# Queries from split half-precision operands, and normalised rows written by GpSimd, in layer 0 of a two-layer decoder kernel

## The reference

```
def _layernorm(x, axis=-1, eps=1e-05):
    m = jnp.mean(x, axis=axis, keepdims=True)
    v = jnp.var(x, axis=axis, keepdims=True)
    return (x - m) / jnp.sqrt(v + eps)
...
    Q = (q @ Wq).reshape(b, N_HEAD, sq, hd_k)
    wei = jnp.einsum('bhqd,bhkd->bhqk', Q, K)
    att = jnp.einsum('bhqk,bhkd->bhqd', jax.nn.softmax(wei, axis=-1), V)
    return out @ Wp
...
    probs = jax.nn.softmax(xf @ router_w.T, axis=-1)
...
x = x + _L0_xattn_ref(_layernorm(x, axis=-1), ctx_1024, ctx_1024, L0_xattn_Wq, L0_xattn_Wk, L0_xattn_Wv, L0_xattn_Wp)
x = x + _L0_ffn_ref(_layernorm(x, axis=-1), L0_ffn_router_w, L0_ffn_w1, L0_ffn_w2)
```

## Time and profile before

| what | value |
|---|---|
| median of 3 runs | 997.5 us (995.8 to 999.16) |
| the profiled execution | 1003.9 us, span 1001.9 us |
| granted TensorE clock, mean of the span | 0.97 of full speed |
| TensorE matmul busy | 918.6 us (92%) |
| VectorE busy | 616.3 us (62%) |
| ScalarE busy | 513.4 us (51%) |
| GpSimd busy | 422.1 us (42%) |

### The profile page before, as it was taken

How to read it: one execution, slowest core, us unless ns; L and a number is a source line. 1 busy time by engine, 2 the same in 40 slices (tenths; PEclk the granted TensorE clock), 3 DMA queues, 4 the chain that set the end, 5 groups by cost and what they waited for, 6 DMA issues and landing times. The chain is left out here.

```text
span 1001.9 us, 23945 instructions
## 1 busy us (share of the span) xinstructions
PE 918.6 (92%) x8022; PEld 640.7 (64%) x8022; DVE 616.3 (62%) x1517; ACT 513.4 (51%) x873; POOL 422.1 (42%) x573
## 2 busy tenths in 40 slices
PE   6799999997458999999999999999989999889995
PEld 4555656554226788898898888888734444454552
DVE  3577888885787434454554545677468888545661
ACT  1478888886352433333333333333456767645663
POOL 2387777772201122334333224553176665204450
PEclk9999999999876999999999999999989999999998
DMA  6423444424541112111111212232143221000112
GB/s 178 89 65 106 114 145 117 141 88 151 154 160 43 44 44 59 43 43 54 54 43 48 60 44 67 90 90 68 33 113 91 81 78 39 2 1 15 51 46 61
DMA packets 73731, 75.46 MB, mean 75 GB/s; under 512 B 22730, under 2 KB 66874, under 8 KB 73626
## 3 DMA queue, kind: packets, MB, share of 16 engines
q1 hardware_dynamic: 67146, 56.31, 18.8%
q0 software_dynamic: 6480, 17.70, 6.7%
HBM read 51.64 MB, written 22.34 MB: 74 GB/s over the span
## 5 line engine op out<-in xcount | busy, mean ns | idle before, releaser
L1925 DVE CAST hh_e<-h_e 128x512 f16<-128x512 f32 x128 | 57.7, 451 | 151.6 <-ACT h_e L1800 87.7
L1564 PE MATMUL banks_ea<-xT_e,experts 128*128 128x256 f16 x512 | 139.6, 273 | 0.0
L1579 PE MATMUL banks_ea<-experts,hh_e 128*128 x512 | 139.6, 273 | 0.0
L1566 PE MATMUL banks_ea<-xT_e,experts 128*128 128x256 f16 x512 | 139.6, 273 | 0.0
L1580 PE MATMUL banks_ea<-experts,hh_e 128*128 x512 | 139.6, 273 | 0.0
L1565 PE MATMUL banks_ea<-xT_e,experts 128*128 128x256 f16 x512 | 139.6, 273 | 0.0
L1578 PE MATMUL banks_ea<-experts,hh_e 128*128 x512 | 139.6, 273 | 0.0
L1800 ACT ACTIVATE h_e<-banks_ea 128x512 f32<-128x512 f32 x128 | 76.4, 597 | 87.3 <-PE banks_ea L1566 87.3
L1383 POOL DMA_INDIRECT x_e<-xh_scratch,token x33 | 36.8, 1114 | 151.5 <-PE banks_ea L1505 105.5
L1927 DVE TENSOR_TENSOR hh_e<-h_e,hh_e 128x512 f16<-128x512 f32 x128 | 88.6, 692 | 4.4
L1854 ACT ACTIVATE experts<-banks_ea 77x1024 f32<-77x1024 f32 x64 | 64.8, 1014 | 41.0 <-PE banks_ea L1673 41.0
(11 more groups left out here) (376 smaller groups left out, 2193.8 us busy)
## 6 DMA issues: line engine op xcount, KB each, us to landing
experts<-in_L_ffn_w SPq DMA_DIRECT2D x22, 512.0 KB, 4.0
y_scratch<-y_e SPq DMA_DIRECT2D x32, 256.0 KB, 3.3
x<-in_x SPq DMA_DIRECT2D x32, 128.0 KB, 3.2
experts<-in_x SPq DMA_DIRECT2D x64, 64.0 KB, 2.4
x_scratch<-x SPq DMA_DIRECT2D x16, 256.0 KB, 2.5
xh_scratch<-xn SPq DMA_DIRECT2D x16, 256.0 KB, 2.7
w_late<-in_L_ffn_w SPq DMA_DIRECT2D x8, 512.0 KB, 4.6
w_late<-x_scratch SPq DMA_DIRECT2D x32, 128.0 KB, 2.6
```

Of the source, the lines that this page charges most:

```text
L1564: mm(out, w[0], xT[0][:, c, :], start=c == 0, stop=False)
L1566: last = mm(out, w[1], xT[0][:, c, :], start=False, stop=c == DC - 1)
L1579: mm(out, a[0], w[1], start=False, stop=False)
```

## The change

The queries are computed in half precision. `wq0` becomes a pair of half-precision tensors, the high part of 64 times the weight (`WSCALE` is 64) and what is left of it; the transposed rows `xT` become a pair too. `queries` adds three products: high rows by high weights, high by low, low by high. That is six matmuls in place of two fp32 ones, which appear as four records in the profile. The low part of the rows is a new VectorE instruction, `low_rows`, which subtracts ScalarE's copy from the PSUM bank; it stands ahead of `result`, and its semaphore `xlo_ok` replaces `xT_ok` wherever TensorE waits. In `prepare`, VectorE makes the pair of weights in two further passes behind the subtraction of the mean. The factor 64 is taken out of the scale `rstd` and of the copy `lx`.

The normalised rows `xn` are written by GpSimd instead of VectorE in the loop: `normed_result` stands behind `deviation` and ahead of the scale for tile k+5. The tiles that are normalised behind the loop stay with VectorE, which waits for GpSimd's part.

```diff
@@ prepare
-                        last = nc.vector.tensor_tensor(G["wq0"][:, :, :], wx[:, :, :],
-                                                       ps[:, None, 0:D + E].broadcast_to([P, DC, D + E]), ALU.subtract)
+                        nc.vector.tensor_tensor(wq[:, :, :], wx[:, :, :],
+                                                ps[:, None, 0:D + E].broadcast_to([P, DC, D + E]), ALU.subtract).then_inc(s_high, 1)
+                        dve.wait_ge(s_high, DC + 1)
+                        nc.vector.tensor_scalar(G["wq0"][:, 0, :, :], wq[:, :, :], WSCALE, None, ALU.mult).then_inc(s_high, 1)
+                        dve.wait_ge(s_high, DC + 2)
+                        last = nc.vector.scalar_tensor_tensor(G["wq0"][:, 1, :, :], wq[:, :, :], WSCALE, G["wq0"][:, 0, :, :],
+                                                              ALU.mult, ALU.subtract)
@@ attend_first, gpsimd
+                def normed_result(n):
+                    pool.wait_ge(rstd1_ok, n + 1)
+                    nc.gpsimd.tensor_scalar(xn[:, n % 4, :], x1[:, n % 4, :], mv1[:, n % 4, 0:1], rstd1[:, n:n + 1],
+                                            ALU.subtract, ALU.mult).then_inc(xn_ok, 1)
+
                     if tile(k - 6):
                         deviation(k - 6)
+                    if tile(k - 6):
+                        normed_result(k - 6)
                     if tile(k + 5):
                         n = k + 5
                         pool.wait_ge(var_ok, n + 1)
-                        nc.gpsimd.tensor_scalar(ve[:, n % 2, :], mv[:, n % 4, 1:2], EPS, None, ALU.add).then_inc(ve_ok, 1)
+                        nc.gpsimd.tensor_scalar(ve[:, n % 2, :], mv[:, n % 4, 1:2], EPS, WSCALE * WSCALE, ALU.add, ALU.mult) \
+                            .then_inc(ve_ok, 1)
@@ attend_first, tensor
                 def high_transposed(f, k):
-                    after(pe, xT_ok, upto(k + 5))
+                    after(pe, xlo_ok, upto(k + 5))
                 def heads_transposed(n, k):
-                    after(pe, xT_ok, upto(k + 6))
+                    after(pe, xlo_ok, upto(k + 6))
                 def rows_transposed(f, k):
-                    after(pe, xT_ok, f)
+                    after(pe, xlo_ok, f)
                 def queries(f, k):
-                    pe.wait_ge(xT_ok, f + 1)
+                    pe.wait_ge(xlo_ok, f + 1)
                     for c in range(DC):
-                        last = mm(q_ps[:, 0:D + E], xT[:, f % 2, flat(c, P)], G["wq0"][:, c, :], start=c == 0, stop=c == DC - 1)
+                        for row, weight in ((0, 0), (0, 1), (1, 0)):
+                            last = mm(q_ps[:, 0:D + E], xT[:, f % 2, row, flat(c, P)], G["wq0"][:, weight, c, :],
+                                      start=c == row == weight == 0, stop=c == DC - 1 and row == 1)
@@ attend_first, scalar
-                        nc.scalar.activation(xT[:, f % 2, :], t_ps[:, 0:D], ACT.Copy).then_inc(xT_ok, 1)
+                        nc.scalar.activation(xT[:, f % 2, 0, :], t_ps[:, 0:D], ACT.Copy).then_inc(xT_ok, 1)
@@ attend_first, vector
-                    nc.vector.tensor_copy(lx[:, f, :], q_ps[:, D:D + E]).then_inc(lx_ok, 1)
+                    nc.vector.tensor_scalar(lx[:, f, :], q_ps[:, D:D + E], 1 / WSCALE, None, ALU.mult).then_inc(lx_ok, 1)
+
+                def low_rows(f):
+                    dve.wait_ge(xT_ok, f + 1)
+                    after(dve, q_done, f - 1)
+                    nc.vector.tensor_tensor(xT[:, f % 2, 1, :], t_ps[:, 0:D], xT[:, f % 2, 0, :], ALU.subtract).then_inc(xlo_ok, 1)
                     if tile(k + 2):
                         maximum(k + 2, 0)
+                    if tile(k + 5):
+                        low_rows(k + 5)
                     if tile(k - 6):
                         result(k - 6)
...
                     if tile(k + 2):
                         maximum(k + 2, 1)
-                    if tile(k - 6):
-                        normed_result(k - 6)
                     if k in CONVERT:
                         weights(CONVERT[k], flat(1, HID // 2))
...
+                    dve.wait_ge(xn_ok, n - 1)
                     normed_result(n - 1)
@@ allocate_first
-    G["wq0"], G["v0"] = L.sb("wq0", [P, DC, D + E]), L.sb("v0_sb", [KEYS, B, HEADS, VW])
+    G["wq0"], G["v0"] = L.sb("wq0", [P, 2, DC, D + E], F16), L.sb("v0_sb", [KEYS, B, HEADS, VW])
-    G["x"], G["xT"] = L.sb("x_0", [P, 8, D]), Q.sb("xT_0", [P, 2, D])
+    G["x"], G["xT"] = L.sb("x_0", [P, 8, D]), Q.sb("xT_0", [P, 2, 2, D], F16)
```

More of the change, by code:

```diff
@@ L188, in prepare @@
         rw = Q.sb("rw", [E, D])
-        wx = Q.sb("wx", [P, DC, D + E])
+        wx, wq = Q.sb("wx", [P, DC, D + E]), Q.sb("wq", [P, DC, D + E])
         mean = Q.sb("mean", [P, P])
@@ L196, in prepare @@
         s_pe, s_act, s_dve, s_v = L.sem("p_pe"), L.sem("p_act"), L.sem("p_dve"), L.sem("p_v")
-        s_k, s_kc, s_wo, s_copies, s_rows, s_mean = (
-            L.sem(f"p_{n}") for n in ("k", "kc", "wo", "copies", "rows", "mean"))
+        s_k, s_kc, s_wo, s_copies, s_high, s_mean = (
+            L.sem(f"p_{n}") for n in ("k", "kc", "wo", "copies", "high", "mean"))
         ident = G["const"][:, CC["ident"][0]:CC["ident"][1]]
@@ L317, in _ @@
                         for c in range(DC):
-                            last = mm(ps[:, 0:E], wpT[:, c, flat(i, P)], G["wq0"][:, c, D:D + E], start=c == 0, stop=c == DC - 1)
+                            last = mm(ps[:, 0:E], wpT[:, c, flat(i, P)], wq[:, c, D:D + E], start=c == 0, stop=c == DC - 1)
                     elif what == "v0":
@@ L401, in _ @@
                     elif what == "k0":
-                        nc.vector.tensor_copy(k0[:, 0, i, :], ps[:, 0:B * KEYS]).then_inc(s_rows, 1)
-                        dve.wait_ge(s_rows, i + 1)
+                        nc.vector.tensor_copy(k0[:, 0, i, :], ps[:, 0:B * KEYS]).then_inc(s_high, 1)
+                        dve.wait_ge(s_high, i + 1)
                         last = nc.vector.tensor_tensor(k0[:, 1, i, :], ps[:, 0:B * KEYS], k0[:, 0, i, :], ALU.subtract)
@@ L521, in attend_first @@
         xr_in, stored = ([L.sem(f"{n}{i}_0") for i in range(2)] for n in ("xr_in", "stored"))
-        ch, var_ok, rstd_ok, rows_done, xT_ok, q_done, qhi_ok, hi2_ok, qlo_ok, lx_ok, lx_out, lx_in = (
-            L.sem(f"{n}_0") for n in ("ch", "var_ok", "rstd_ok", "rows_done", "xT_ok", "q_done", "qhi_ok", "hi2_ok",
+        ch, var_ok, rstd_ok, rows_done, xT_ok, xlo_ok, q_done, qhi_ok, hi2_ok, qlo_ok, lx_ok, lx_out, lx_in = (
+            L.sem(f"{n}_0") for n in ("ch", "var_ok", "rstd_ok", "rows_done", "xT_ok", "xlo_ok", "q_done", "qhi_ok", "hi2_ok",
                                       "qlo_ok", "lx_ok", "lx_out", "lx_in"))
@@ L1001, in _ @@
                         weights(LENT_CHUNKS + 1 + i)
+                dve.wait_ge(xn_ok, NT - 1)
                 normed_result(NT - 1)
```

## The result

The median went from 998.33 us (995.8 to 999.45) to 1020.45 us (1017.42 to 1022.22), four executions each: a ratio of 1.0221, 95% interval 1.0194 to 1.0249, so 22 us slower (19.4 to 24.9). The profiled execution took 1020.47 us with a span of 1018.7. The forecast was slower by 5.8 us, at 1003, with a range up to 1011: the direction held, the size did not, and the range missed the time.

What follows compares the result with a forecast made beforehand. Before, the ScalarE-TensorE loop set short steps and TensorE long ones; after, loop B would. 10 x 6.33 + 11 x 6.70 = 137.0 against 131.5, +5.5, plus 0.3 preparation: +5.8 us, 1003; range 994.5 to 1011.

Steps and rivals of the forecast that it cites:

- Loop B: Per-step cycle from ScalarE's `high` through VectorE and GpSimd to the next `high`; 5.34 us of work, forecast 6.33 without weights.
- TensorE's saving: Queries as six half-precision matmuls, 0.66 us for 0.97: 0.31 us a step, worth at most 3.3 us.
- The failed step: Length of GpSimd's new normalised-rows pass in the loop: taken as 0.45 us, 0.42 delaying the next instruction; ends 0.33 and 0.72.
- The rule's estimate: GpSimd's pass priced by VectorE being about twice as fast elementwise: some 0.8 us, the whole at about 1011.
- The wait for `heads_out`: VectorE's `heads` waiting for TensorE in long steps: 0.55 us before, 0.06 on average left after the change.
- The factor in the variance: Factor added to the variance instruction, counted as replacing an instruction one for one: nothing.
- Steps with weights: In 11 of 21 intervals, VectorE's expert-weight conversion and GpSimd exclude each other: 0.37 us more, 6.70; upper end 0.75.
- Preparation: Two more VectorE passes behind `mean` in `prepare` delay the wide key matmuls: +0.3 us.
- the pass that costs as much as a two-input one, with conflicts: Rival, chance 0.12: GpSimd's pass takes 0.72 us or more; +15 with full conflicts, +11 with half, 1009 to 1012.
- TensorE's saving arrives: Rival, chance 0.16: loop B stays under loop A, so the shorter queries bring the time to 993.5 to 994.5.
- loop A: Per-step cycle of ScalarE's exponentials and TensorE's matmuls, without `queries`: 6.0 us in short steps, 6.2 in long ones after.
- The 21 intervals: Times between starts of ScalarE's `high` in layer 0's attention, tile 10 to 31: 131.48 us before, 137.0 forecast.

Runs made afterwards that it cites:

- e4: Kernel before the change, with ten unused GpSimd instructions of several kinds and sizes added in the preparation to price them; 994.64 us, one execution.
- e3: Kernel before the change, with only the normalised-rows pass moved to GpSimd, ahead of the scale, queries still fp32; 1009.65 us, ratio 1.010.
- e7: Changed kernel with a plain GpSimd copy in place of the normalisation pass, so rows stay unnormalised; 1012.68 us, ratio 1.0143.
- e1: Changed kernel with GpSimd's normalised-rows pass moved behind the scale for tile k+5; 1002.0 us, ratio 1.0037.
- e2: Changed kernel with the normalised-rows pass back on VectorE, so the half-precision queries alone; 1001.73 us, ratio 1.002.
- second pair: Changed kernel and kernel before, both unaltered, each profiled a second time; 1017.51 and 998.74 us, one execution each.
- e8: Changed kernel with GpSimd's scale for tile k+5 ahead of both `deviation` and the pass, plus idle TensorE matmuls; 1001.28 us, ratio 1.0038.

## Why the prediction was right in direction and wrong in size

*The bound.* Right. Loop B sets the step after the change, no longer told apart by the mask, with ScalarE idle ahead of `high` until the scale. TensorE's saving arrives nowhere: the queries take 0.69 us to the next transposes (160.02 to 160.71; 0.66 predicted, 0.97 in the earlier trace rows; the 0.27 that the prediction reads as one matmul alone is in the earlier trace rows a record of two of 128 columns, and its price came out all the same) and TensorE then stands idle, 0.84 us ahead of the `x` transposes.

*The failed step.* "Its length is not in the trace. [...] It has one tensor input and two column scalars, so I take 0.45 [...]; ends 0.33 and 0.72." The pass takes 1.24 us, outside both ends. The bounds were casts and a two-input operation, and the instruction was placed between them by its number of inputs; e4 shows that on this engine the kind of instruction sets the price. It delays the next one by 1.21 (e3) and not by 0.42. On its own that term is worth 21 x 0.79 = 16.6 us, more than the whole gap of 149.25 - 137.0 = 12.3; the other terms below gave 4.3 back in sum. The Trainium skill (GPSIMD Engine Reference, section 8, Key points) has VectorE about twice as fast for elementwise work; the trace disagrees with the size, 1.24 against 0.40 for this pass being 3.1. The rule's estimate, 0.8 and a time of 1011, was still the better guide than the casts.

*The other terms of loop B.* Nearly right: e7, with the pass at 0.40, has 137.68 for 137.0, in part because two misses cancel. `low_rows` is 0.33 for 0.37. The wait for `heads_out` is gone (L955 starts at 156.12 with no idle time ahead of it) where 0.06 was left in. The factor in the variance was put at nothing, as an instruction replaced one for one, and costs 0.08 a step.

*Steps with weights.* Right in mechanism, not for this pass. Beside VectorE's second half GpSimd's scale is held by 0.5 us in e7, in every step with weights, and by 0.4 in two steps of e1. In the changed kernel nothing is: the long pass runs from 152.86 to 154.11 over the weights' second half (153.54 to 154.21), both at their usual length, and the scale starts at 154.18. So all intervals are 7.09, and the 0.37 in 11 of them, 4.1 us, was not paid.

*Preparation.* +0.3 was predicted, and the wide key matmuls do wait; the timeline of the changed kernel, for the earlier trace rows:

```profile
23.03 0.48 DVE L433 TENSOR_TENSOR kc<-prep_ps,kc 128x308 f16<-128x308 f32 x1
...
23.56 0.38 PEld L338 LDWEIGHTS prep_ps<-experts 128*128 128x128 f16 x4 [0.35 <-DVE kc L433]
```

But from the first context matmul (L331) to the first `x` transposes it is 27.55 us, 27.66 before: nothing arrives.

*The rivals.* The nearest was the pass that costs as much as a two-input one, with conflicts, at 1009 to 1012: right in that the pass is longer, wrong in the conflicts, and still too short by half. (By its own sum, 997.5 + 15.4 + 0.3, it ends at 1013.) The rival "TensorE's saving arrives" is what e2 shows, without the pass: loop B under loop A, intervals 1.8 us shorter in sum, no gain in the time.

*The sum.* The median is longer by 22 us (19.4 to 24.9). The 21 intervals account for 17.8 in the first pair of profiles and 17.6 in the second; where the rest of the 22 lies is open. The first pair is only 16.6 us apart: 3.2 more lie in the tail, with the clock, and 4.2 less behind the start of the routing (724.2 against 728.4). The second pair is 18.8 apart: 1.6 more ahead of tile 10's `high`, 1.3 less in the tail, 1.0 more behind the start of the routing. Whether the change makes the tail's lower clock more frequent is open.

## What to carry to other kernels

Before work goes to another engine, look for a row of that very instruction there, not of a cheaper kind of the same size; without one, the upper end of the price is open, and the question is what waits behind it in the queue. An instruction whose result is needed late belongs behind those whose result is needed now: here one swap was worth 18 us. Two halves of a change that share a loop are priced together: the queries' half took 1.8 us off the intervals or added 6.8, depending on the other half.

## What the runs showed of the hardware that was not expected

- GpSimd's `tensor_scalar` on 128x256 in fp32 takes 0.93 to 1.23 us (e4), dearer than a two-input subtraction (0.73) and two to three times a copy (0.40). A product by a column takes 0.93 as `tensor_scalar` (L297) and 0.61 as a two-input operation with the column broadcast (L295).
- A GpSimd `tensor_scalar` on one column starts 0.03 us before the instruction ahead of it ends if it has one operation, and 0.08 after if it has two (before and e1, e3 and the changed kernel).
- VectorE's weight pass, with two SBUF inputs, and GpSimd hold each other up. Short GpSimd instructions that start while it runs end 0.04 to 0.10 after it (`tensor_scalar`, 0.51 for 0.19 in e8) or 0.40 to 0.43 after it (the power, 1.06 for 0.55 in e7), and the long pass, started 0.11 into it, takes 1.69 for 1.24 (e1). Where GpSimd's wide products (L630) were running, VectorE's pass itself took 0.96 to 1.36 for 0.67 (e8). But a GpSimd pass of 1.24 us that had begun 0.7 to 0.8 us earlier ran beside it, and neither was longer than alone (the changed kernel, e3).
- With the shorter queries the clock fell to 0.50 early in the stage in e1, e2 and e7, but in neither profile of the changed kernel, although TensorE is less busy there (4.33 us of the 6 from 60 to 66 us, against 4.75 in e2). In e2 its longest wait from 50 us to the fall is 1.17 us; the changed kernel has one of 1.18 us at much the same place, and no fall. What decides it these rows do not show.
